# Probabilities transposed in place, graph convolutions with tiles of their own, and new instruction orders

## The reference

```python
def layernorm(x): return (x - mean(x)) / sqrt(var(x) + 1e-5)

# layer 0: attention over the graph, masked by adj
w = adj * exp(q @ k.T);  x0 = layernorm(x + (w / w.sum()) @ v)
# layer 1: three graph convolutions
z = relu(adj @ (x0 @ W1) + b1); z = relu(adj @ (z @ W2) + b2)
x1 = layernorm(x0 + adj @ (z @ W3) + b3)
# layer 2: hypergraph convolution to 512 features, relu, layer norm, back to 256
h = layernorm(relu(Dn * H @ (Be * H.T @ (x1 @ Wup)) + bup)) * gamma + beta
x2 = layernorm(x1 + (x1 + Dn * H @ (Be * H.T @ (h @ Wdown)) + bdown))   # H = (adj != 0)
# layer 3: attention with 8 heads of 32; scores times (adj + adj)
p = softmax(2 * adj * (q @ k.T) / sqrt(32))
x3 = layernorm(x2 + (p @ v) @ Wo + bo)
```

## Time and profile before

| | before |
|---|---|
| median of 3 runs | 1071.79 us (1071.34 to 1073.0) |
| profiled execution | 1069.87 us, span 1068.1 us |
| PE busy | 1029.0 us, 96% of the span |
| DVE, ACT, POOL busy | 833.6 (78%), 649.7 (61%), 480.1 us (45%) |
| chain that ended last | PE 90%, DVE 5%, ACT 3% |
| granted TensorE clock, mean over the span | 0.993 |
| memory traffic | 43.35 MB, 41 GB/s |

### The profile page before, as it was taken

How to read it: one execution, slowest core, us unless ns; L and a number is a source line. 1 busy time by engine, 2 the same in 40 slices (tenths; PEclk the granted TensorE clock), 3 DMA queues, 4 the chain that set the end, 5 groups by cost and what they waited for, 6 DMA issues and landing times.

```text
span 1068.1 us, 21761 instructions
## 1 busy us (share of the span) xinstructions
PE 1029.0 (96%) x8412; PEld 912.8 (85%) x8412; DVE 833.6 (78%) x2216; ACT 649.7 (61%) x1755; POOL 480.1 (45%) x298
## 2 busy tenths in 40 slices
PE   8799999999999999999999999999999999998865
PEld 7689898888989888898989888898988889896754
DVE  4666878788787878878787887978788797877765
ACT  3445755839385683948567384846748484763624
POOL 2135362645435364543535464354546435451713
PEclk9999999999999999999999999999999999999988
DMA  6110102001010100101010110101011010000001
GB/s 227 50 60 9 62 2 70 21 30 60 30 61 11 61 21 30 60 31 60 12 60 21 37 54 30 60 11 64 24 44 41 31 60 11 31 2 11 21 1 40
DMA packets 17384, 43.35 MB, mean 41 GB/s; under 512 B 2049, under 2 KB 2049, under 8 KB 17153
## 3 DMA queue, kind: packets, MB, share of 16 engines
q1 hardware_dynamic: 17280, 41.97, 11.4%
HBM read 33.57 MB, written 8.39 MB: 39 GB/s over the span
## 4 chain that ended last, share of the span: by engine, by line
PE 90%; DVE 5%; ACT 3%; issue 1%; DMA 0%; POOL 0%; POOLq 0%; SPq 0%; DVEq 0%
PE ps L470 82%; PE ps L782 5%; PE ps L723 1%; ACT pr L942 1%; DVE pr L1239 1%; PE ps L573 1%; PE ps L653 1%; DVE x L1124 0%; DVE mx L1244 0%; DMA pr<-in_weights 0%; DVE st L1062 0%; ACT fT_high L879 0%; DVE fT_rest L1142 0%; ACT up_high L919 0%; ACT upT L922 0%
## 5 line engine op out<-in xcount | busy, mean ns | idle before, releaser
L1371 POOL TENSOR_TENSOR pr<-pr,den 128x1024 f32<-128x1024 f32 x64 | 121.6, 1902 | 86.2 <-DVE den L1259 86.0
L942 ACT ACTIVATE pr<-pr,mx 128x128 f32<-128x128 f32 x384 | 149.4, 406 | 9.7 <-DVE mx L1244 9.6
L1325 POOL TENSOR_TENSOR rstd<-var,neg_half 128x4 f32<-128x4 f32 (+1 forms) x84 | 73.3, 873 | 111.6 <-DVE var L1073 110.1
L1078 DVE TENSOR_SCALAR x<-x,mv,rstd 128x256 f32<-128x256 f32 x256 | 91.1, 416 | 34.1 <-POOL rstd L1325 33.9
L1350 POOL TENSOR_TENSOR x<-x,rows 128x1024 f32<-128x1024 f32 x16 | 38.1, 2380 | 170.2 <-PE ps L470 170.2
L1062 DVE BATCH_NORM_STATS2 st<-x 128x6 f32<-128x256 f32 x256 | 92.3, 412 | 1.1
L1239 DVE TENSOR_TENSOR pr<-ps,adjB 128x1024 f32<-128x1024 f32 x64 | 75.2, 1217 | 14.5 <-PE ps L470 14.5
L896 ACT COPY s_s<-ps 128x512 f32<-128x512 f32 x32 | 18.8, 587 | 105.4 <-PE ps L470 105.4
L1360 POOL TENSOR_TENSOR hv<-hv,neg_half 128x2 f32<-128x2 f32 x32 | 22.5, 704 | 129.4 <-DVE hv L1205 129.4
L942 ACT ACTIVATION_READ_ACCUMULATOR pr<-pr,mx 128x1 f32 x384 | 78.7, 205 | 0.0
L1057 DVE TENSOR_TENSOR fT_rest<-ps,fT_high 128x512 fp32r<-128x512 f32 x96 | 62.9, 681 | 20.2 <-ACT fT_high L932 14.4
(11 more groups left out here) (198 smaller groups left out, 3267.4 us busy)
## 6 DMA issues: line engine op xcount, KB each, us to landing
xT<-in_xT SPq DMA_DIRECT2D x16, 512.0 KB, 3.3
x<-in_x SPq DMA_DIRECT2D x16, 512.0 KB, 3.2
out_x<-x SPq DMA_DIRECT2D x32, 256.0 KB, 2.0
adjA<-in_adj SPq DMA_DIRECT2D x16, 256.0 KB, 2.9
adjTA<-in_adjT SPq DMA_DIRECT2D x16, 256.0 KB, 2.7
adjB<-in_adj SPq DMA_DIRECT2D x16, 256.0 KB, 2.6
pr<-in_weights SPq DMA_DIRECT2D x2, 512.0 KB, 6.0
qkT<-in_weights SPq DMA_DIRECT2D x1, 1024.0 KB, 11.8
```

The source lines that it names most:

```text
L942: act.activation(pr[:, b, k, :], pr[:, b, k, :], ACT.Exp, bias=mx[:, b, k:k + 1], accum_out=den[:, b, 0, k:k + 1]).then_inc(exp_ready, 1)
L1078: dve.tensor_scalar(t[:, b, :], t[:, b, :], mv[i][:, b, 0:1], rstd[i][:, b:b + 1], ALU.subtract, ALU.mult).then_inc(ready, 1)
L1325: pool.tensor_tensor(rstd[i][:, bs], var[i][:, bs], neg_half[:, bs], ALU.pow).then_inc(rstd_ready[i], len(pairs))
L1371: pool.tensor_tensor(pr[:, b], pr[:, b], den[:, b, 1, :].unsqueeze(2).broadcast_to([P, HEADS, P]), ALU.mult).then_inc(pr_ready, 1)
```

## The change

Three edits go together:

- The copies of the transposed probabilities go back into `pr[:, b]`, over the probabilities of the same graph, and `mha_ctx` reads them there. `prT` is gone. The set-up's `rep` moves into `x2` and `x3`, which are free then.
- The graph convolutions get the tiles `aT_high` and `aT_rest`; `fT_high` and `fT_rest` are left to the stages B and C. `e0` and `p0` become one tile.
- All tables of steps have new orders. The steps are the same ones, but for `keep_busy`: 5 instead of 6 in the prologue, 9 instead of 4 in the epilogue (each four matmuls).

```diff
@@ tables (two of many lines of the loop's PE list)
-        ("C", "mha_turn1"), ("A", "gcn_1"), ("C", "mha_ctx0"), ("A", "gcn_1_rest"), ("C", "mha_turn2"),
-        ("C", "mha_wo0_high"), ("A", "gcn_2s1_high"), ("A", "gcn_2s0_high"), ("C", "mha_wo0"), ("A", "gcn_2s0"),
...
-        pr = sb("pr", [P, GB, HEADS, P]); prT = sb("prT", [P, 2, HEADS, P])
+        pr = sb("pr", [P, GB, HEADS, P])
...
-        x2T = gxT = axT = z_high = sb("fT_high", [P, C, N4], F32R)
-        fT_rest = sb("fT_rest", [P, C, N4], F32R)
+        axT = z_high = sb("aT_high", [P, C, N4], F32R)
+        x2T = gxT = sb("fT_high", [P, C, N4], F32R)
+        aT_rest = sb("aT_rest", [P, C, N4], F32R); fT_rest = sb("fT_rest", [P, C, N4], F32R)
...
-        e0 = sb("e0", [P, GB, P]); p0 = sb("p0", [P, GB, P])
+        e0 = p0 = sb("e0_p0", [P, GB, P])
...
-        rep = prT[:].rearrange("p t h n -> p (t h) n")
+
+        def rep(k):
+            return (x2, x3)[k // 8][:].rearrange("p b (c n) -> p (b c) n", c=C)[:, k % 8, :]
...
                             last = mm(ps4[j * DH:(j + 1) * DH, 4 + 2 * pair, 2 * i + bb], v3[:, b, h * DH:(h + 1) * DH],
-                                      prT[:, bb, 2 * j + i, :])
+                                      pr[:, b, 2 * j + i, :])
...
             def mha_turn(g, b):
                 act.wait_ge(prT_done, GB * g + b + 1)
-                act.copy(prT[:, b % 2, 0:4, :], ps4[:, turn_bank(b)]).then_inc(prT_act, 1)
+                act.copy(pr[:, b, 0:4, :], ps4[:, turn_bank(b)]).then_inc(prT_act, 1)
...
-            def residue(g, c, bank, high_part, high_ready, ready):
+            def residue(g, c, bank, high_part, high_ready, part_rest, ready):
                 dve.wait_ge(high_ready, C * g + c + 1)
-                dve.tensor_tensor(fT_rest[:, c, :], ps[:, bank + c, :], high_part[:, c, :], ALU.subtract).then_inc(ready, 1)
+                dve.tensor_tensor(part_rest[:, c, :], ps[:, bank + c, :], high_part[:, c, :], ALU.subtract).then_inc(ready, 1)
...
             def mha_turn(g, b):
                 dve.wait_ge(prT_done, GB * g + b + 1)
-                dve.tensor_copy(prT[:, b % 2, 4:8, :], ps4[:, turn_bank(b) + 1]).then_inc(prT_dve, 1)
+                dve.tensor_copy(pr[:, b, 4:8, :], ps4[:, turn_bank(b) + 1]).then_inc(prT_dve, 1)
```

More of the change, by code:

```diff
@@ L511, in set_att @@
                 for o in range(C):
-                    last = mm(ps[:, 4, 0:1], rep[:, o, :], bk0[:, o, :], o, C)
+                    last = mm(ps[:, 4, 0:1], rep(o), bk0[:, o, :], o, C)
                 last.then_inc(att_mm, 1)
@@ L518, in set_down @@
                 for f in range(HC):
-                    mm(ps[:, 5, 0:D], rep[:, C + f, :], w_down[:, f, 0:D], f, HC)
+                    mm(ps[:, 5, 0:D], rep(C + f), w_down[:, f, 0:D], f, HC)
                 for f in range(HC):
-                    last = mm(ps[:, 6, 0:D], rep[:, 2 * C + HC + f, :], w_down[:, f, 0:D], f, HC)
+                    last = mm(ps[:, 6, 0:D], rep(2 * C + HC + f), w_down[:, f, 0:D], f, HC)
                 last.then_inc(down_mm, 1)
@@ L527, in set_wo @@
                 for o in range(C):
-                    last = mm(ps[:, 7, 0:D], rep[:, C + HC + o, :], w_o[:, o, :], o, C)
+                    last = mm(ps[:, 7, 0:D], rep(C + HC + o), w_o[:, o, :], o, C)
                 last.then_inc(wo_mm, 1)
@@ L602, in gcn_1_rest @@
                     for c in range(C):
-                        last = rest_pass(ps[:, m, :], "W1", slice(m * P, (m + 1) * P), fT_rest, c)
+                        last = rest_pass(ps[:, m, :], "W1", slice(m * P, (m + 1) * P), aT_rest, c)
                     last.then_inc(z1_done, 1)
@@ L613, in gcn_2s @@
                 pe.wait_ge(z1_rest, C * g + C)
-                rest_rows(ps2[:, 2 + pair, 0], "W2", fT_rest, graph(2 * pair))
+                rest_rows(ps2[:, 2 + pair, 0], "W2", aT_rest, graph(2 * pair))
                 high_rows(ps2[:, 2 + pair, 1], "W2", z_high, graph(2 * pair + 1))
-                rest_rows(ps2[:, 2 + pair, 1], "W2", fT_rest, graph(2 * pair + 1)).then_inc(s2_done, 1)
+                rest_rows(ps2[:, 2 + pair, 1], "W2", aT_rest, graph(2 * pair + 1)).then_inc(s2_done, 1)
             def gcn_2a(g):
@@ L632, in gcn_3s @@
                 pe.wait_ge(z2_rest, C * g + C)
-                rest_rows(ps2[:, 2 + pair, 0], "W3", fT_rest, graph(2 * pair))
+                rest_rows(ps2[:, 2 + pair, 0], "W3", aT_rest, graph(2 * pair))
                 high_rows(ps2[:, 2 + pair, 1], "W3", z_high, graph(2 * pair + 1))
-                rest_rows(ps2[:, 2 + pair, 1], "W3", fT_rest, graph(2 * pair + 1)).then_inc(s3_done, 1)
+                rest_rows(ps2[:, 2 + pair, 1], "W3", aT_rest, graph(2 * pair + 1)).then_inc(s3_done, 1)
             def gcn_3a(g, pair):
@@ L1010, in set_rep @@
                 for c in range(C):
-                    last = dve.tensor_scalar(rep[:, c, :], ones[:], bq0[:, c, :], None, ALU.mult)
+                    last = dve.tensor_scalar(rep(c), ones[:], bq0[:, c, :], None, ALU.mult)
                 last.then_inc(rep_ready, 1)
@@ L1133, in mha_xt @@
             def mha_xt(g, c):
-                residue(g, c, 6, x2T, x2T_ready, x2T_rest)
+                residue(g, c, 6, x2T, x2T_ready, fT_rest, x2T_rest)
             def hyper_rest(g, c):
-                residue(g, c, 6, gxT, gx_ready, gx_rest)
+                residue(g, c, 6, gxT, gx_ready, fT_rest, gx_rest)
             def z_rest(g, m, full, rest_ready):
                 dve.wait_ge(full, C * g + m + 1)
-                dve.tensor_tensor(fT_rest[:, m, :], ps[:, m, :], z_high[:, m, :], ALU.subtract).then_inc(rest_ready, 1)
+                dve.tensor_tensor(aT_rest[:, m, :], ps[:, m, :], z_high[:, m, :], ALU.subtract).then_inc(rest_ready, 1)
             def gcn_1(g, m):
@@ L1155, in gcn_ax @@
             def gcn_ax(g, c):
-                residue(g, c, 2, axT, ax_ready, ax_rest)
+                residue(g, c, 2, axT, ax_ready, aT_rest, ax_rest)
             def incidence(g):
```

27 lines of the change are left out of this document (13 added, 14 removed), and 253 rows, old and new, of tables (EPILOGUE, PROLOGUE, SCHEDULE).

## The result

| | before | changed |
|---|---|---|
| median of the runs | 1071.79 us | 1065.86 us (1064.95 to 1066.7) |
| ratio, 95% interval | | 0.9942 [0.9928, 0.9957] |
| span of the profiled execution | 1068.1 us | 1064.2 us |
| granted clock, mean over the span | 0.993 | 0.998 |

The change makes the kernel 5.9 us faster, where 2.1 us were forecast and 1066.0 was the low end of the range. The two profiled executions lie only 3.9 us apart. So there are two things to explain: why the traces differ by 3.9 us and not by 2.1, and where the timed runs have 2 us more.

What follows compares the result with a forecast made beforehand. TensorE's own stream was taken to bound the loop, with waits and low clock outside it. Terms -0.5 + 1.0 - 0.2 - 1.4 - 1.0 = -2.1 us took 1071.8 to 1069.7 us; range 1066.0 to 1074.0.

Steps and rivals of the forecast that it cites:

- The tiles: New and shared tiles, probabilities written back into `pr`: no instruction added, put at 0.
- A: Prologue: one `keep_busy` goes and a wait for `fT_rest` ends, -0.5 us.
- B: Loop: one more switch to the split type a turn, 0.08 us each, +1.0 us over 12 turns.
- C: Last group's hypergraph output: VectorE's reordered scalings and addition let the transposes end earlier, -0.2 us.
- D: Last group's first projections at full clock behind filling products: seven spacings of 0.43 become 0.23 us, -1.4 us.
- E: Last projection at full clock through more `keep_busy`: 11 spacings shrink from 0.21 to 0.12 us, -1.0 us.
- R2: Rival, last group but one: normalisation beside GpSimd's addition shrinks from 3.22 to 0.73 us, 2.5 us gained; chance 0.20.
- R3: Rival, loop: PE waits for one scaling more, 0.44 us a turn, 5.3 us lost; chance 0.15.
- R4: Rival, last group: the 16 filling products themselves run at low clock, 4.6 us lost, 1074.3 us; chance 0.05.

Runs made afterwards that it cites:

- tiles_only: The changed kernel with all three tables of orders of the kernel before; median 1072.03 us, ratio 1.0004 to the kernel before.
- pool_behind: The changed kernel with GpSimd's old list around the last group but one; one execution, last product at 202.62 us against 200.32 in the changed kernel.
- no_fills: The changed kernel with none of the epilogue's new `keep_busy`, the old one put back; median 1067.32 us, ratio 0.9964 to the kernel before.
- last_group: The changed kernel with a new order of VectorE, PE and ScalarE steps in the last group alone; median 1065.63 us, ratio 0.9948 to the kernel before.
- split_v: The changed kernel with VectorE's maximum between two masks (last two groups), `mha_v` between the last group's scores; median 1065.99 us, ratio 0.9953 to before.
- old_y: The changed kernel with VectorE's old order of variance, scalings and additions in the last two groups; median 1066.42 us, ratio 0.9955 to before.

## Why the prediction was wrong

- **The tiles: right.** Nothing by themselves (tiles_only).
- **A, the prologue, -0.5: right.** Counted from the start, PE reaches turn 3's `att_scores` 0.37 us earlier in the trace (176.86 against 177.23), but traces with one and the same prologue differ by over 1 us there, since the set-up ends earlier or later. Counted from the first `att_scores` they differ by 0.1 us at most, and the new prologue is 0.47 us shorter.
- **B, +1.0: mis-sized.** It measured at most 0.3 us over the loop. The count was right: in the traces a turn has 14 changes into the split type, 13 before, and the first spacing behind one is 0.28 us in the mean, against 0.15 us between two split products, with either order. But the other spacings of the turn are shorter by nearly as much in sum. A single wider spacing was taken for the price of a change, and it is not.
- **C, -0.2: right in size.** The end of `mha_xt` gained 1.59 - 1.29 = 0.3 us over the end of `hyper_out` 15 (162.38 before, 161.09 after, counted as in the table).
- **D, -1.4: right between these two traces.** From the end of `mha_xt` to `mha_scores0` it is 8.71 against 7.33 us. 0.5 of it needs VectorE's new order too, as far as the rows tell.
- **E, -1.0: right.** From `mha_wo1_high` to the end it is 1.93 us instead of 2.81, 0.9 less.
- **The step that failed first: nothing was counted for the last group but one.** I had its idle time and the 3.22 us beside GpSimd's work, made it the rival R2, and left it out of the sum. It measured 1.35 us: 0.7 from PE's order of `gcn_3s` and `gcn_3a`, and 0.65 that no run isolates, where GpSimd's list has a part. The place was R2's. Its mechanism, a shorter normalisation that PE waits for, was not: the normalisation is down to 0.73 us (at 985.64), but VectorE's `mha_shift3` beside GpSimd's addition takes 3.22 us now, and PE waits for neither. What mattered was when the division is done, by its place in GpSimd's queue and by what it meets there (pool_behind). The Trainium skill states a lock on ports that VectorE and GpSimd share, held for a whole instruction ("SBUF — State Buffer", section "SBUF: two separate sides"). The trace agrees: the 3.22 us of `mha_shift3` beside an addition, the 2.88 us of pool_behind's division beside `mha_shift3`.
- **The step that failed second: "the median of the runs shown lies 1.9 us above that execution, and with the same difference the forecast is 1069.7".** The difference was no constant. It was mostly the length of low clock that this one execution happened to lack, in the stretches that D and E take away. D and E in a trace like that of tiles_only are 4.3 us instead of 2.3: `mha_scores0` comes 4.27 us earlier in the changed kernel, 1.67 of it up to the transposes, so D is 2.6; from there to the last product 1.7 more. That makes 206.30 - 200.32 = 6.0 us behind `att_scores` 14, and the timed runs have 5.9 and, again, 5.8 in all. The traces show what the fillings do in an execution with long stretches. How the timed gain divides between order and fillings stays open, because no_fills, without them, kept 3.9 us.

Between the two traces the parts add up: A -0.46, the loop +0.29, up to the end of `hyper_out` 15 -1.29, C -0.30, D -1.38 and E -0.88 us are -4.02, and the set-up ended 0.08 later, against 3.9 us measured. Of the 3.8 us by which the forecast missed, about 1.3 are the last group but one, 0.7 the loop, and the rest the added 1.9.

R3 and R4 did not come true: no wait appeared in the loop, and the fillings start 0.24 us apart (3.85 us for 16, from 1018.62 to 1022.47).

## What to carry to other kernels

When the median lies above the profiled execution by as much as the effect looked for, ask in which stretch the others lose it before the difference is added as a constant: compare mean clocks, and trace a second execution, since a mean also counts what lies behind the last product. Where engines other than TensorE set the pace (here the last two groups), go through each queue for work that stands ahead of what TensorE waits for, and for what that work will meet on another engine: two additions ahead of a division used up 3.8 us of slack here, and the meeting behind them cost PE 1 us. When a piece is put back to price it, look at the granted clock behind the new wait before the whole delay is given to the piece. To cancel differences of the set-up, count from an instruction behind it. And a shorter chain may pay only together with fillings in the idle times it leaves: last_group alone gained nothing in the runs.

## What the hardware showed that I had not expected

The same program had its clock at 0.50 behind the same idle time for 3.4 us in one execution and for 6.8 us in another (before and tiles_only, with one order), and the whole times fall into two groups, 1.6 us apart in their medians, as the mean clocks do. The clock fell behind single idle times of 1.93 us (pool_behind) and 2.12 us (split_v). In old_y's trace the granted clock stood at 0.95 for nearly the whole span, and a turn of the loop was only 0.4% longer for it (62.17 against 61.91 us). What sets either is open.
